# A macaron layer with routed experts: stores held two tiles back, the router judged inside attention's loop, weight splitting and additions moved

## The reference

```python
x = x + 0.5 * ffn(layernorm(x))      # x: 1024 tokens x 256
x = x + attn(layernorm(x))
x = x + 0.5 * ffn(layernorm(x))

# ffn: a shared expert with a gate, and the 4 best of 16 routed experts
shared = (silu(x @ Gs.T) * (x @ Us.T)) @ Ds.T * sigmoid(x @ sgate.T)   # 704 wide
p = softmax(x @ gate.T);  w, ids = top_k(p, 4)
for e in range(16):
    coef = sum(where(ids == e, w, 0))
    acc += ((silu(x @ G[e].T) * (x @ U[e].T)) @ W2[e].T) * coef        # 176 wide
out = shared + acc

# attn: gated linear attention, 2 heads of 128, in chunks of 64
q = silu(x @ Wq.T); f = sigmoid(x @ Wk.T); log_f = log_sigmoid(f); v = x @ Wv.T
S_t = diag(f_t) S_{t-1} + outer(k_t, v_t);  o_t = q_t @ S_t            # k = 1 - exp(log_f)
out = rmsnorm(o, norm_w) @ Wo.T
```

## Time and profile before

| | us |
|---|---|
| median of 3 runs (lowest, highest) | 455.74 (454.93, 457.75) |
| the profiled execution's own time | 455.48 |
| its span on the core | 453.7 |
| PE busy | 410.8 (91% of the span) |
| DVE busy | 300.4 (66%) |
| ACT busy | 202.1 (45%) |
| POOL busy | 188.9 (42%) |

### The profile page before, as it was taken

One profiled execution on the slowest core, in us unless ns is written; L12 is line 12 of the kernel. 1 busy time (PEld: TensorE's weight loads), 2 busy tenths in 40 slices (PEclk: granted clock), 3 DMA queues, 4 the chain that ended last, 5 costly groups with the idle time before them and its releaser, 6 DMA issues.

```text
span 453.7 us, 8744 instructions
## 1 busy us (share of the span) xinstructions
PE 410.8 (91%) x2236; PEld 330.4 (73%) x2239; DVE 300.4 (66%) x943; ACT 202.1 (45%) x564; POOL 188.9 (42%) x199
## 2 busy tenths in 40 slices
PE   5998993699999999978969989689989999999995
PEld 3555552599999999553649975355569999999954
DVE  5666986377777776367596545645767777777637
ACT  2224562266666666124755632001126666666610
POOL 0174846044445445330055300767514544544542
PEclk9988997699999999989998976989999999999999
DMA  7999941344444441660000029422244444444167
GB/s 248 332 281 386 344 136 66 105 136 139 136 148 137 138 144 66 245 252 2 0 0 1 1 73 372 170 104 103 79 119 137 136 138 148 132 145 141 68 242 258
DMA packets 41023, 68.17 MB, mean 150 GB/s; under 512 B 5072, under 2 KB 32208, under 8 KB 40976
## 3 DMA queue, kind: packets, MB, share of 16 engines
q1 hardware_dynamic: 33392, 45.84, 32.4%
q0 software_dynamic: 7584, 21.77, 13.6%
HBM read 42.42 MB, written 25.17 MB: 149 GB/s over the span
## 4 chain that ended last, share of the span: by engine, by line
PE 70%; issue 7%; POOL 6%; DVE 6%; DMA 6%; ACT 3%; SPq 1%; DVEq 0%; POOLq 0%
PE ps L486 7%; PE ps L487 7%; PE ps L490 7%; POOL slots L907 6%; PE ps L426 6%; PE ps L449 5%; PE ps L471 5%; PE ps L431 4%; PE ps L519 3%; PE ps L514 2%; PE ps L518 2%; PE ps L516 2%; PE ps L515 2%; PE ps L497 2%; PE ps L498 2%
## 5 line engine op out<-in xcount | busy, mean ns | idle before, releaser
L914 POOL DMA_INDIRECT rows<-ar,idx x94 | 89.8, 955 | 118.0 <-ACT ar L762 117.4
L907 POOL DMA_INDIRECT slots<-XR,pos x64 | 70.1, 1096 | 76.5 <-DVE pos L1084 41.6
L486 PE MATMUL ps<-WH,xt 128*128 x188 | 69.2, 369 | 0.0
L487 PE MATMUL ps<-WL,xt 128*128 x188 | 61.1, 327 | 0.0
L1127 DVE SCALAR_TENSOR_TENSOR ar<-ps,XR,ar 128x112 f32<-128x112 f32 x94 | 31.4, 334 | 37.9 <-ACT ar L756 37.7
L1143 DVE TENSOR_TENSOR xl<-ps,xt 128x256 fp32r<-128x256 f32 x94 | 39.9, 424 | 24.2 <-ACT xt L751 10.6
L449 PE MATMUL ps<-WS,ar 128*128 128x256 f32 (+1 forms) x192 | 48.4, 399 | 8.1 <-DVE ar L996 7.4
L449 PEld LDWEIGHTS ps<-WS,ar 128*128 128x128 f32 (+1 forms) x192 | 37.3, 197 | 24.7 <-issue 12.9
L756 ACT ACTIVATE ar<-ps 128x176 f32<-128x176 f32 x94 | 29.9, 318 | 51.5 <-PE ps L490 51.5
L426 PE MATMUL ps<-XT,WS 128*128 128x512 f32 x96 | 50.8, 656 | 1.0 <-ACT sgt L739 1.0
L745 ACT ACTIVATE ar<-ps 128x512 f32<-128x512 f32 (+1 forms) x24 | 14.3, 596 | 80.3 <-PE ps L426 80.3
(11 more groups left out here) (171 smaller groups left out, 855.3 us busy)
## 6 DMA issues: line engine op xcount, KB each, us to landing
XR<-slots SPq DMA_DIRECT2D x94, 144.0 KB, 2.1
WR<-w SPq DMA_DIRECT2D x8, 1408.0 KB, 17.1
WR<-rows SPq DMA_DIRECT2D x16, 512.0 KB, 7.3
slots<-zeros SPq DMA_DIRECT2D x1, 2304.0 KB, 12.6
MR<-w2r SPq DMA_DIRECT2D x2, 1024.0 KB, 19.3
MR<-w2m SPq DMA_DIRECT2D x1, 1792.0 KB, 14.3
rows<-ar,idx POOLq DMA_INDIRECT x94, 2.4
X<-x SPq DMA_DIRECT2D x4, 256.0 KB, 4.6
```

The source lines that it names most:

```text
L486: pe.matmul(to, token, WH[:, bass.ds(e, 1), k, :].rearrange("p a n -> p (a n)"), start=k == 0, stop=False)
L487: pe.matmul(to, token, WL[:, bass.ds(e, 1), k, :].rearrange("p a n -> p (a n)"), start=False, stop=False)
L907: pool.indirect_dma_start(out=slots_dram[:, :], out_offset=bass.IndirectOffsetOnAxis(ap=pos[:, t, r:r + 1], axis=0), in_=XR[:, t, :], in_o ...
L914: pool.indirect_dma_start(out=rows_dram[:, :], out_offset=bass.IndirectOffsetOnAxis(ap=idx[:, i:i + 1], axis=0), in_=ys[i % NY], in_offset ...
```

## The change

The stores to `slots` count on two semaphores by the tile's parity, and tile t waits only for the stores of tile t - 2. In `ffn(0)` DVE works out the first half's `pos` ahead of norming tiles 4 to 7. PE's `ranks` and `over_partitions`, and DVE's `choose`, `places`, `tiles_of` and `tables`, move by one unit against the shared expert's work. `keep_warm` ahead of the slots runs in both passes. W2's blocks 4 to 16 are split in two pieces behind unit 8: on ACT ahead of its slot loop, on DVE in turn 0 of the slot loop. `shared_sums` of the second half moves behind the first `left` of DVE's slot loop, in both passes. `judge(1, 0)` and `router(1, 0)` move into attention's loops.

```diff
@@ -23,7 +23,7 @@
 FE, FS = 176, 704
 
 W2_FIRST = {2: (0, 8), 3: (8, NE)}
-W2_LAST = {7: (0, 4), 8: (4, NE)}
+W2_LAST = {7: (0, 4), 8: (4, 10), 9: (10, NE)}
 PARTED = {3: (0, 2), 4: (2, 5), 5: (5, 8), 6: (8, 11), 7: (11, 14), 8: (14, NE)}
 
 FM = 112
@@ -43,9 +43,6 @@
 
 NX, NY = 6, 4
 AHEAD = 8
-
-
-BREAKS = (3, 6)
 
 
 PAIRED = (0, 1, 6, 7)
@@ -237,9 +234,10 @@
         s_w2r, s_rh, s_rl, s_w2m, s_mh, s_ml = (sem(n) for n in "s_w2r s_rh s_rl s_w2m s_mh s_ml".split())
         s_set = sem("s_set")
         s_mv, s_ln, s_rs, s_xn, s_tp, s_xc = (sem(n) for n in "s_mv s_ln s_rs s_xn s_tp s_xc".split())
-        s_lg, s_lgc, s_ex, s_sgx, s_sel, s_rank, s_pos, s_disp, s_dg, s_tp4, s_tab, s_chain = (
-            sem(n) for n in "s_lg s_lgc s_ex s_sgx s_sel s_rank s_pos s_disp s_dg s_tp4 s_tab s_chain".split())
+        s_lg, s_lgc, s_ex, s_sgx, s_sel, s_rank, s_pos, s_dg, s_tp4, s_tab, s_chain = (
+            sem(n) for n in "s_lg s_lgc s_ex s_sgx s_sel s_rank s_pos s_dg s_tp4 s_tab s_chain".split())
         s_ug, s_uu, s_usi, s_uh, s_u2, s_xsh = (sem(n) for n in "s_ug s_uu s_usi s_uh s_u2 s_xsh".split())
+        s_disp = [sem(f"s_disp{b}") for b in range(2)]
         s_xs = [sem(f"s_xs{i}") for i in range(NX)]
         s_tx, s_xtc, s_l1, s_sil, s_hm, s_ht, s_hh, s_hl, s_l2, s_y = (
             sem(n) for n in "s_tx s_xtc s_l1 s_sil s_hm s_ht s_hh s_hl s_l2 s_y".split())
@@ -354,7 +352,8 @@
                     for e in range(0, NE, 4):
                         sp.dma_start(WR[:, e:e + 4, :, :], w13[e:e + 4].rearrange("e k p n -> p e k n")).then_inc(s_we[e // 4], 16)
                 sp.wait_ge(s_tab, f + 1)
-                sp.wait_ge(s_disp, 16 * NT * TOPK * (f + 1))
+                for b in range(2):
+                    sp.wait_ge(s_disp[b], 16 * TOPK * HT * (f + 1))
                 for i in range(TL):
                     at = start_of(i)
 
@@ -411,7 +410,7 @@
                 pe.wait_ge(s_dg, f + 1)
                 pe.matmul(table_at, ones[:, :], dg[:, :, :].rearrange("p c i -> p (c i)"), start=True, stop=True).then_inc(s_tp4, 1)
 
-            def unit_in(f, u):
+            def unit_in(f, u, between=None):
                 h, j = u // NJ, u % NJ
                 if u == 0:
                     pe.wait_ge(s_ws, 32)
@@ -426,6 +425,8 @@
                     mm = pe.matmul(ps[:, 4 + u % 2, :], WS1[:, k, 2 * j, :], XT[:, k, half(h)],
                                    start=k == 0, stop=k == KD - 1)
                 mm.then_inc(s_ug, 1)
+                if between:
+                    between()
                 if not last:
                     for k in range(KD):
                         mm = pe.matmul(ps[:, 6 + u % 2, :], WS1[:, k, 2 * j + 1, :], XT[:, k, half(h)],
@@ -527,8 +528,7 @@
                             turned(0, t)
                         if t > 0:
                             logits(0, t - 1)
-                unit_in(f, 0)
-                ranks(f, 0)
+                unit_in(f, 0, lambda: ranks(f, 0))
                 if f == 0:
                     for t in range(HT, NT + 1):
                         if t < NT:
@@ -537,16 +537,17 @@
                             logits(0, t - 1)
                 unit_in(f, 1)
                 unit_out(f, 0)
+                unit_in(f, 2)
                 ranks(f, 1)
-                unit_in(f, 2)
                 unit_out(f, 1)
+                unit_in(f, 3)
+                unit_out(f, 2)
                 over_partitions(f)
-                for u in range(3, FRONT):
+                for u in range(4, FRONT):
                     unit_in(f, u)
                     unit_out(f, u - 1)
                 unit_out(f, FRONT - 1)
-                if f == 1:
-                    keep_warm(8, 6)
+                keep_warm(8, 6)
 
                 pe.wait_ge(s_tab, f + 1)
                 slot_turn(f, 0)
@@ -782,15 +783,15 @@
                     act.wait_ge(s_w2r, 32)
                     some = slice(*W2_FIRST[u])
                     act.activation(RH[:, some, :], MR[:, some, :], ACT.Copy).then_inc(s_rh, 1)
-                if u in W2_LAST:
-                    act.wait_ge(s_w2m, 16)
-                    some = slice(*W2_LAST[u])
-                    act.activation(MH[:, some, :], MR[0:FM, some, :], ACT.Copy).then_inc(s_mh, 1)
-
                 for e in range(*PARTED.get(u, (0, 0))):
                     if e % 4 == 0:
                         act.wait_ge(s_we[e // 4], 16)
                     act.activation(WH[:, e, :, :], WR[:, e, :, :], ACT.Copy).then_inc(s_wh, 1)
+
+            def main(u):
+                act.wait_ge(s_w2m, 16)
+                some = slice(*W2_LAST[u])
+                act.activation(MH[:, some, :], MR[0:FM, some, :], ACT.Copy).then_inc(s_mh, 1)
 
             def ffn(f):
                 if f == 0:
@@ -800,7 +801,12 @@
                 for u in range(FRONT):
                     unit(f, u)
                     if f == 0:
+                        if u == 7:
+                            main(u)
                         part(u)
+                if f == 0:
+                    main(8)
+                    main(9)
                 slots(f)
                 for u in range(FRONT, UNITS):
                     unit(f, u)
@@ -884,7 +890,8 @@
                 decays(3)
                 for i in range(3, NT + 5):
                     step(i)
-                router(1, 0)
+                    if i == NT + 2:
+                        router(1, 0)
 
             act.preload_act_table_set("natural_log_exp_and_others")
             act.wait_ge(s_set, 1)
@@ -900,13 +907,11 @@
                 for h in range(2):
                     pool.wait_ge(s_pos, 2 * f + h + 1)
                     for t in range(HT * h, HT * (h + 1)):
-                        if t in BREAKS:
-
-                            pool.wait_ge(s_disp, 16 * TOPK * (NT * f + t))
+                        wait(pool, s_disp[t % 2], 16 * TOPK * (HT * f + t // 2))
                         for r in range(TOPK):
                             pool.indirect_dma_start(
                                 out=slots_dram[:, :], out_offset=bass.IndirectOffsetOnAxis(ap=pos[:, t, r:r + 1], axis=0),
-                                in_=XR[:, t, :], in_offset=None).then_inc(s_disp, 16)
+                                in_=XR[:, t, :], in_offset=None).then_inc(s_disp[t % 2], 16)
 
             def results(f):
                 for i in range(TL):
@@ -998,6 +1003,13 @@
                     ins = dve.tensor_tensor(Hs[u % 2][0:LAST, :], ps[LAST:P, 4 + u % 2, :], Sg[u % 2][0:LAST, :], ALU.mult)
                 ins.then_inc(s_uh, 1)
 
+            def main(u):
+                dve.wait_ge(s_mh, list(W2_LAST).index(u) + 1)
+                for e in range(*W2_LAST[u], 2):
+                    two = slice(e, e + 2)
+                    ins = dve.tensor_tensor(ML[:, two, :], MR[0:FM, two, :], MH[:, two, :].bitcast(F32), ALU.subtract)
+                ins.then_inc(s_ml, 1)
+
             def part(f, u):
                 if f == 0 and u in W2_FIRST:
                     dve.wait_ge(s_rh, list(W2_FIRST).index(u) + 1)
@@ -1005,12 +1017,8 @@
                         two = slice(e, e + 2)
                         ins = dve.tensor_tensor(RH[FR:P, two, :], MR[FR:P, two, :], RH[FR:P, two, :].bitcast(F32), ALU.subtract)
                     ins.then_inc(s_rl, 1)
-                if f == 0 and u in W2_LAST:
-                    dve.wait_ge(s_mh, list(W2_LAST).index(u) + 1)
-                    for e in range(*W2_LAST[u], 2):
-                        two = slice(e, e + 2)
-                        ins = dve.tensor_tensor(ML[:, two, :], MR[0:FM, two, :], MH[:, two, :].bitcast(F32), ALU.subtract)
-                    ins.then_inc(s_ml, 1)
+                if f == 0 and u == 7:
+                    main(u)
                 for e in range(*PARTED.get(u, (0, 0))):
                     if f == 0:
                         dve.wait_ge(s_wh, e + 1)
@@ -1145,13 +1153,18 @@
                 dve.wait_ge(s_tab, f + 1)
                 left(0)
                 e = list(experts_from(0, mybir.EngineType.DVE))
+                shared_sums(f, 1, FRONT)
                 for i in range(TL + 1):
                     if i + 1 < TL:
                         if len(e) == i + 1:
                             e.extend(experts_from(i + 1, mybir.EngineType.DVE))
                         left(i + 1)
+                    if f == 0 and i == 0:
+                        main(8)
                     if i < TL:
                         hidden(i, e[i])
+                    if f == 0 and i == 0:
+                        main(9)
                     if 1 <= i <= TL:
                         rest(i - 1)
 
@@ -1221,20 +1234,22 @@
             def ffn(f):
                 if f == 0:
                     judge(f, 1)
+                unit(f, 0)
                 choose(f, 1)
-                unit(f, 0)
+                unit(f, 1)
                 places(f, 1)
                 tiles_of(f)
-                unit(f, 1)
-                tables(f)
-                for u in range(2, NJ + 1):
```

(11 more changed lines are left out.)

## The result

The forecast was 444.2 us; the changed kernel took **481.13 us** (474.85 to 489.79, 4 runs), the kernel before 455.34 (454.6 to 457.75, 4 runs) on the same chip. The ratio is 1.044, 95% interval 1.036 to 1.051: slower, where 0.975 was forecast. The profiled execution took 474.85.

A forecast was written before the change was run, and what follows sets the result against it. PE's idle gap before the slots was the bound, its end set by POOL's dispatch of stores. 455.48 less 7.4 (first pass) and 4.1 (second) gave 444.0, or 444.2 us at the median's level; range 441 to 450.

The forecast's parts named there:

- Stores two tiles behind: POOL's dispatch: waiting only for tile t - 2 removes the second pass's stops, 2.9 us, and leaves 2 us in the first.
- The rival on the slower side: POOL at tiles 2 to 7, first pass: six waits for landing stores instead of two, 457.9 us; 5%.
- the 4% for "slower": Chance given to the changed kernel being slower by over 1%, from the tail of the six-waits rival.
- First store: First pass, POOL: pos no longer stands behind the four scalings, so the first store starts at 19.85 instead of 21.14.
- Stops of the first pass: POOL's waits for landed stores in the first dispatch: 2 us in all, ends 0 and 16.2.
- Stores that last longer: Dispatch: long or late stores beside DVE's weight subtractions cost 7 us in the first pass, 4.1 in the second.
- What the slot loop takes over: DVE behind left(0): sums and two ML pieces make the first output product 2.2 us later; first pass nets 7.4.
- Second pass: Earlier router and ranks, first store at 281.3, slots at 329.8: 5.1 us gained, less 1.0 for shared_sums, net 4.1.
- with the units 2 us sooner and no stop: Lower bound of the forecast: PE's shared-expert units end 2 us earlier and POOL has no stop, 441.5 us.
- The long stores: POOL's dispatch: a store of 2.91 us instead of 0.96, put beside DVE's subtractions, resting on one row's neighbourhood.

The follow-up runs named there:

- experiment 2: Changed kernel with the second half's shared_sums and W2's last two pieces on DVE put back ahead of the slots: 434.15 us, 0.963 of the kernel before.
- the control: The kernel before, unaltered, run again on chip 5 for its trace: 450.94 us, 1.003.
- the run on chip 2: The kernel before, unaltered, profiled again on an undisturbed chip: 448.99 us, 0.998, with 6,868 updates.

## Why the prediction was wrong, and where it was right

**The step that failed is "Stores two tiles behind"**, the second pass: "no stop, 2.9 us gone". It counted a stop as POOL's own time and nothing else, and the whole part priced the unbroken run of stores at nothing for the other engines, without naming that as an assumption. On chip 15 the increments that DVE and ACT wait for come up to 22.9 us late without the stops and up to 9.3 with them, and the kernel takes 482.4 us instead of 454.3. The price in the result's run, against the same kernel on chip 5: second dispatch 71.7 instead of 46.7, 25.0 us; first output product of the first pass at 92.88 instead of 85.47, 7.4 us; attention 1.8; the rest under 1 together. 33.5 in all, the difference of the spans 473.0 and 439.4. None of my rivals was this one. The rival on the slower side put the loss on POOL's waits; POOL's last stores were at 64.2 and 319.4, earlier than the forecast's 68.0 and 324.6. The range and the 4% for "slower" left it out.

Could the profile have told? The trace of before has no "remote" release and all its updates, so no row in it was a warning. What was at hand is that the stops might serve something else than the stores' landing; I asked only what a stop costs POOL, and not what happens meanwhile on the engines that it lets alone.

**Where signals come in time, the mechanism held and the sum nearly did**: 9.2 us (chip 7) and 9.3 us (chip 5) gained of 11.5 forecast, 0.979 and 0.976 for 0.975. That it comes so close is in part luck, for two things that it missed worked against each other: the pause ahead of the 29th store goes, which gained some 2 us in the second pass, and the end is longer, which cost 1.7. POOL's timeline of the changed kernel on chip 5, first pass:

```profile
20.05 1.11 POOL L912 DMA_INDIRECT slots<-XR,pos  x1 [19.60 <-DVE pos L1092]
...
30.98 0.96 POOL L912 DMA_INDIRECT slots<-XR,pos  x1 [0.97 <-DMA slots<-XR,pos]
...
54.30 2.51 POOL L912 DMA_INDIRECT slots<-XR,pos  x1 [0.30 <-issue]
57.11 2.60 POOL L912 DMA_INDIRECT slots<-XR,pos  x1 [0.30 <-issue]
...
64.17 0.96 POOL L912 DMA_INDIRECT slots<-XR,pos  x1 [0.30 <-issue]
```

and PE's, where the second pass's slots begin:

```profile
313.63 1.89 PE L381 MATMUL ps<-warm 128*128 128x512 bf16 x8
317.53 0.41 PE L472 MATMUL ps<-cst,XR 128*128 128x128 f32 x2 [2.01 <-issue]
```

Step by step, against the kernel before on the same chip:

- *First store*: 19.85 forecast, 20.05. *Stops of the first pass*: 2 us forecast, one of 0.97 (it stands in the fence, at the ninth store, tile 2).
- *Stores that last longer*: 7 us forecast, 4.0. The forecast took its 7 out of 8.6 us of "stores that last longer or start late", and 2.0 of those 8.6 were POOL's pause ahead of the 29th store, which the second semaphore removes. So the last store came at 64.2 instead of 68.0, and PE alone set the start: slots at 74.58, 73.9 forecast.
- *What the slot loop takes over*: 2.2 forecast; from slots to first output product 10.9 instead of 7.8, so 3.1. The first pass gained 7.0 net (92.51 to 85.47), 7.4 forecast. The working charged the loop for this work as if there were no other place; experiment 2 shows that ahead of the loop it fits, for DVE waits there anyway, and gains 5.7 over both passes.
- *Second pass*: the dispatch took 46.7 instead of 51.4, 4.6 gained where 2.9 was forecast. The forecast kept all 4.1 us of late and long stores; 2.0 of them were the pause ahead of the 29th store, now gone, and the rest stayed (2.3 in place of 2.0). The first store came only 0.7 sooner after the end of the first slots (94.2 instead of 94.9 us behind it) where 2.1 was forecast; together 5.4 for 5.1. The first output products then came 1.4 later from the slots' start, for 1.0.
- *Not in the sum*: from the last output product to the end, 23.9 us instead of 22.2. Nine traces of versions with the new order show 23.6 to 24.8, one (without the first pass's fillers) 22.0; the kernel before has 22.2, 22.2 and 22.9. I did not find why.

The parts of the spans: -7.0 first pass, +0.3 slots, -0.7 attention, -4.6 dispatch, +1.4, +0.1 and +1.7 come to -8.9 before rounding, from 448.3 to 439.4. One sum of the forecast is off: with the units 2 us sooner and no stop, its terms give 444.2 - 2.0 = 442.2, not 441.5; nothing else hangs on it.

**The long stores** were put down to DVE's subtractions beside them, by one row of before. On chip 5 it looks so: DVE's timeline there has

```profile
53.28 2.69 DVE L1028 TENSOR_TENSOR WL<-WR,WH 128x352 fp32r<-128x352 f32 x6
...
56.62 2.69 DVE L1028 TENSOR_TENSOR WL<-WR,WH 128x352 fp32r<-128x352 f32 x6
```

around the stores of 2.51 and 2.60. But in the result's run six such subtractions, at 58.70, had stores beside them that took little more than their 0.96:

```profile
58.70 2.69 DVE L1028 TENSOR_TENSOR WL<-WR,WH 128x352 fp32r<-128x352 f32 x6
```

```profile
58.88 1.17 POOL L912 DMA_INDIRECT slots<-XR,pos  x1 [0.30 <-issue]
60.35 1.01 POOL L912 DMA_INDIRECT slots<-XR,pos  x1 [0.30 <-issue]
```

So the subtraction alone does not make a store long. The Trainium skill, "SBUF — State Buffer", section "Who interferes with whom", expects that tensor_tensor should not hold up GpSimd's descriptors, which it marks as inferred; the stores of 1.17 and 1.01 us agree with it, those of 2.51 and 2.60 do not, and what else it takes stays open.

**Shown and not shown.** Shown: the stores alone bring the loss (482.2 against 457.8), the missing stops do and the second semaphore does not (482.4 and 454.3 on one chip), the new order is needed neither for the loss nor for the gain of 0.975; most of the gain is the missing stops', some 3.4 us the second semaphore's. Not shown: by what path a stream of stores holds back another engine's increment, whether a stop helps by its pause or by waiting until the stores have landed, whether the stream of weight loads has a part in it (it runs beside both dispatches), why some chips are free of it, and whether the kernel before has late signals on the disturbed ones. On the stops: POOL's pause of 2.34 us ahead of the 29th store, at 325.04 to 327.38 in the kernel without stops, ended none of the waits, and of the six "remote" waits in the second pass of the kernel with stops one ended inside a stop, at 307.29.

A rival stands untested: each run on record comes with a span and a clock of the profiler, and the disturbed traces lack records, so the recording itself may have a part in the lateness; no run here is without it.

Two numbers speak for late signals in the kernel before: it takes 455.5 to 457.8 us on chips 4 and 15 and 448.7 to 449.6 on the four others, and the kernel with two semaphores and the old stops, which takes as long (1.002), loses 7.6 us in its second dispatch (59.0 for 51.4). Against it stands the profile ahead of the prediction, 455.48 us and no late signal; its span is 5.4 us over the control's on chip 5, and the attention alone is 6.6 longer (101.5 us from the last product of the first slots to the next store, for 94.9), with a granted clock of 0.82 in its last 43 us where the run on chip 2 had 1.00 in its last 41.

## What to carry to other kernels

A stop in a stream of DMA issues costs its engine what the profile says, but it may also be what keeps other engines' signals from coming late. Before taking it out, ask what else shares the way with that stream, and give "the stream itself is what the stops hold down" a price as a rival. Time such a change on several chips: here the new stores alone take 0.975 and 0.984 of the time on two of them and 1.056 on a third. When two things change in one place, here the waits and the number of semaphores, run each by itself: the one that seemed free moved 3.4 us. And before moving work from in front of a loop into it, look for idle time of its engine ahead of the loop: work that fits there (here DVE's) costs the path nothing, and inside the loop it did.

## What the runs showed of the hardware

- On chips 4 and 15 (and in the result's run), while GpSimd issues an indirect store of 128 rows every 1.26 us, increments of TensorE arrive at VectorE and ScalarE up to 28 us late (up to 9.3 with the two stops), in the result's run in clumps about 10 us apart in the second dispatch (305.7, 316.2, 325.4). In the five traces without the old stops they are all through 4 to 6 us after the second dispatch's last store starts (319.38 to 325.4; 314.05 to 319.9; 316.51 to 322.5; 328.84 to 334.7; 331.18 to 335.2). In the slot loop, with a store about every 2 us, no wait of VectorE or ScalarE was over 1.4 us.
- The same traces hold 4,630 to 4,910 of some 6,860 semaphore updates. A trace's own completeness was thus a mark of the disturbance, in all six traces that had late increments and in none of the fourteen others.
- On chips 5, 7 and 13 the same stores at the same pace do nothing of the kind.
- With one semaphore for all 32 stores of a pass, GpSimd is idle for 2.34 to 2.38 us ahead of the 29th in both passes, in all seven traces of such kernels; with two semaphores, in thirteen traces, it is idle there for at most 0.35 us unless a wait for landed stores held it.
